# K, V and the first two contexts of cross attention are computed inside the last bodies of self attention

## The chip, the cores and the metric

The kernel runs on one core of a Trainium2 chip. The time is device microseconds (us) of one execution of the whole program. The program has three phases one after the other: self attention, cross attention, MLP. Each phase is a block of its own with its own semaphores; at the end of a block all engines meet at a barrier.

## The reference

```python
x_norm = modulate(_ln(x), shift_a, scale_a)          # x: (16, 224, 512)
q, k, v = split(x_norm @ W_qkv + b_qkv)              # 16 heads of 32
attn_out = softmax(q k^T * scale) v @ W_proj + b_proj
x = x + gate_a * attn_out
q_c = _ln(x) @ W_qc + b_qc
k_c, v_c = split(_ln(context) @ W_kvc + b_kvc)       # context: (16, 750, 512)
x = x + (softmax(q_c k_c^T * scale) v_c) @ W_cproj + b_cproj
x_norm2 = modulate(_ln(x), shift_m, scale_m)
x = x + gate_m * (gelu(x_norm2 @ W_mlp1 + b_mlp1) @ W_mlp2 + b_mlp2)
```

`k_c` and `v_c` depend only on the context and on W_kvc, so they need nothing of self attention.

## The kernel before, in words

Every product of the projections is made of three float32r matmuls (high times low, low times high, high times high; `product`, L71 to L73), so each operand is kept as a high part, rounded by ScalarE (ACT), and a low part, the difference, made by VectorE (DVE).

**Self attention** works through one batch of 16 after the other. `bodies` calls `body` with c = 0 to 18, and each engine has its own `body`, a loop over 16 steps h, one for each head. Body c computes the attention of batch c, and between its heads the filling work of the table `FILL`: K, Q, V of batch c+1, the output projection ("p") of batch c-1, the cross query ("c") of batch c-2 and transposes ("tx", "ty"). A head's second scores, its exponentials and its part of P·V come six heads late (`LAG`). Body 15 is the last with heads of its own and has no K, Q or V to fill with; body 16 finishes the heads of batch 15 and its output projection; body 17 turns the last x for the cross query, and its last product runs at the start of body 18. The row maxima of four heads are turned by TensorE (PE, L473), split by DVE (L708, L710) and written by a DMA of SyncE (SP, `place_maxima`, L301) as two more rows of the stacked Q; only then may the second scores (L485) of these heads run. Behind body 18 SP waits for all stores of `x1` and `qc`, and the barrier follows.

In body 14 SP loads W_kvc (`load_wkv`), in body 15 ACT and DVE split it (`high_wkv` L875, `low_wkv` L679), and SP loads context 0 into `c_in`, whose statistics DVE takes at the end of body 15 (L683). ACT normalizes it in body 16 (L879).

**Cross attention** first has a stretch of its own: six tiles of context 0 are transposed (L1336) and split (L1615, L1504), then `FIRST`: eight halves of K (four groups of four heads, each in two halves of 376 and 374 keys) and six tiles of V, with the six tiles of context 1 between the V. K is copied by SP into `kst` (`stack_k` L1270: twelve DMAs a group; three rows of parts, high, low, high), and `qc` into `qst` (`load_q` L1263: three DMAs a group). GpSimd (POOL) fills the two rows of ones of `kst` with one MEMSET (L1706). Then come the scores of head 0 (L1375) and bodies 0 to 16, made like those of self attention, with K and V of batch c+1 and the tiles of context c+2 as filling. The second scores are L1389, six heads late and again behind `place_maxima` (L1278). SP's order in front of body 0 is: Q and K of the four groups, six tiles of context 2, then the maxima of group 0.

Each engine runs its instructions in the order in which they are written; nothing is scheduled. A wait stands in the engine's own queue and holds up all behind it.

## Time and profile before

| | |
|---|---|
| median of 3 runs | 2712.4 us (2710.79 to 2716.66) |
| profiled execution | 2714.79 us, its span 2712.8 us |
| PE busy | 2616.2 us, 96% |
| DVE, ACT, POOL busy | 63%, 42%, 48% |
| PE's mean granted clock | 0.978 |
| body 15 begins, about | 678 us |
| last product of self attention ends | 760.3 us |
| first PE instruction of cross attention | 768.0 us |
| scores of cross head 0 | 812.2 us |
| first second scores of cross attention | 831.5 us |
| MLP begins, about | 1945 us |

The span runs from the first to the last instruction that the profiler recorded. A row of a timeline has the start in us, the duration in us, the engine, the line and the operation with its output and inputs; what stands in brackets is how long the engine had been idle before, and what ended that. The granted clock ("PEclk") is the share of TensorE's full speed (2.4 GHz) that was granted in a stretch: 1.00 is all of it, 0.50 is 1.2 GHz throughout.

### The profile page before, as it was taken

The numbers are of one execution on the slowest core, as the hardware profiler recorded it, in microseconds if no ns is written. First come the engines' busy times: TensorE is split into PE (matmuls) and PEld (weight loads), VectorE is DVE, ScalarE is ACT, GpSimd is POOL, SyncE is SP. The second block draws the span as 40 slices with busy tenths as digits, with TensorE's granted clock in tenths as the row PEclk, the third lists the DMA queues.
The fourth block names the chain that finished last, engine by engine and source line by source line (L and its number), as shares of the span: only waits on it lengthen the run. The fifth ranks groups of instructions, "written<-read, shape, count | busy, mean of one in ns | idle before, by whom it ended". The sixth has DMA issues, their size and how long they took to land. (4 is left out here: it accounts for less than half of the span.)

```text
span 2712.8 us, 49884 instructions
## 1 busy us (share of the span) xinstructions
PE 2616.2 (96%) x18548; PEld 2150.8 (79%) x18548; DVE 1708.4 (63%) x3413; ACT 1126.3 (42%) x2187; POOL 1303.5 (48%) x1447
## 2 busy tenths in 40 slices
PE   8899999999789999999999999999799999999997
PEld 6688888888578888888888888887478888888886
DVE  6677777776727777777777777776654444444431
ACT  4354444444434555555555555554432212212210
POOL 1445445454415777777777777767611221220211
PEclk9999999999889999999999999999799999999999
DMA  7454545545243444444444444334231111111110
GB/s 221 127 131 118 130 124 137 129 117 153 85 131 98 113 113 112 109 112 113 118 113 111 111 120 117 107 89 124 83 113 36 43 47 36 43 47 36 43 43 24
DMA packets 190609, 269.86 MB, mean 99 GB/s; under 512 B 32769, under 2 KB 110593, under 8 KB 190353
## 3 DMA queue, kind: packets, MB, share of 16 engines
q1 hardware_dynamic: 187296, 259.33, 35.4%
q0 software_dynamic: 3072, 7.34, 0.8%
q8 instruction: 149, 2.44, 0.4%
q14 instruction: 92, 0.75, 0.1%
HBM read 111.11 MB, written 36.77 MB: 55 GB/s over the span
## 5 line engine op out<-in xcount | busy, mean ns | idle before, releaser
L1639 ACT ACTIVATE cross_prT<-cross_tr_ps 125x448 f32<-125x448 f32 x768 | 407.4, 544 | 285.0 <-PE cross_tr_ps L1389 275.9
L1517 DVE TENSOR_REDUCE cross_parts<-cross_sc_ps 112x1 f32<-112x500 f32 x512 | 336.9, 664 | 213.3 <-PE cross_sc_ps L1375 212.0
L1690 POOL TENSOR_TENSOR cross_part<-cross_prT 125x448 f32<-125x448 f32 x252 | 291.7, 1157 | 212.8 <-PE cross_or_ps L1409 113.7
L1013 POOL TENSOR_TENSOR self_psum<-self_prT 112x224 f32<-112x224 f32 x256 | 180.9, 707 | 331.0 <-ACT self_prT L903 321.0
L1389 PE MATMUL cross_tr_ps<-cross_qst,cross_kst 98*125 98x224 f32 x1536 | 312.7, 287 | 3.8 <-ACT cross_prT L1639 3.3
L1389 PEld LDWEIGHTS cross_tr_ps<-cross_qst,cross_kst 98*125 98x125 f32 x1536 | 256.7, 189 | 62.0 <-ACT cross_prT L1639 23.3
L1692 POOL TENSOR_TENSOR cross_part<-cross_part,cross_prT 125x448 f32<-125x448 f32 x252 | 291.5, 1157 | 19.8
L2087 ACT ACTIVATE mlp_hv<-mlp_h_ps,mlp_b 128x512 f32<-128x512 f32 x112 | 76.9, 687 | 520.1 <-PE mlp_h_ps L73 506.1
L1375 PE MATMUL cross_sc_ps<-cross_kst,cross_qst 96*112 96x500 f32 (+1 forms) x1024 | 262.6, 337 | 3.2 <-DVE cross_parts L1517 3.0
L2004 DVE CAST mlp_hT_h<-mlp_hv 128x512 fp32r<-128x512 f32 x112 | 53.4, 477 | 320.0 <-ACT mlp_hv L2087 320.0
L903 ACT ACTIVATE self_prT<-self_st_ps 112x448 f32<-112x448 f32 x256 | 138.2, 541 | 187.3 <-PE self_st_ps L485 186.9
L1375 PEld LDWEIGHTS cross_sc_ps<-cross_kst,cross_qst 96*112 96x112 f32 x1024 | 164.2, 178 | 19.0 <-DVE cross_parts L1517 4.3
L1694 POOL TENSOR_TENSOR cross_psum<-cross_part 125x224 f32<-125x224 f32 x252 | 169.8, 674 | 19.7
L71 PE MATMUL mlp_a_ps<-mlp_w_l,mlp_hT_h 128*128 128x512 f32 x448 | 178.3, 398 | 0.0
L701 DVE TENSOR_REDUCE self_nmax<-self_sc_ps 112x2 f32<-112x448 f32 x256 | 154.4, 613 | 36.9 <-PE self_sc_ps L456 36.9
L72 PE MATMUL mlp_h_ps<-mlp_xT_h,mlp_w_l 128*128 128x512 f32 x448 | 177.5, 396 | 0.0
L72 PE MATMUL mlp_a_ps<-mlp_w_h,mlp_hT_l 128*128 128x512 f32 x448 | 176.9, 395 | 0.0
L1402 PE MATMUL cross_or_ps<-cross_prT,cross_vt 125*32 125x224 f32 x3072 | 167.5, 369 | 9.7 <-DVE cross_ou L1548 9.0
L73 PE MATMUL mlp_h_ps<-mlp_xT_h,mlp_w_h 128*128 128x512 f32 x448 | 176.7, 395 | 0.0
L73 PE MATMUL mlp_a_ps<-mlp_w_h,mlp_hT_h 128*128 128x512 f32 x448 | 176.6, 394 | 0.0
L71 PE MATMUL mlp_h_ps<-mlp_xT_l,mlp_w_h 128*128 128x512 f32 x448 | 176.6, 394 | 0.0
L1519 DVE TENSOR_REDUCE cross_parts<-cross_sc_ps 112x2 f32<-112x500 f32 x256 | 170.2, 665 | 0.0
(274 smaller groups left out, 6742.2 us busy)
## 6 DMA issues: line engine op xcount, KB each, us to landing
cross_kst<-cross_nat_h SPq DMA_DIRECT2D x512, 93.8 KB, 2.2
cross_c_in<-in_context SPq DMA_DIRECT2D x96, 250.0 KB
cross_kst<-cross_nat_l SPq DMA_DIRECT2D x256, 93.8 KB, 2.2
cross_qst<-qc SPq DMA_DIRECT2D x192, 112.0 KB, 2.5
self_kst<-self_nat_h SPq DMA_DIRECT2D x128, 112.0 KB, 2.3
self_qst<-self_natq_h SPq DMA_DIRECT2D x128, 112.0 KB, 3.0
self_x_in<-in_x SPq DMA_DIRECT2D x16, 448.0 KB, 3.8
self_kst<-self_nat_l SPq DMA_DIRECT2D x64, 112.0 KB, 2.3
```

Source lines behind the costliest of these rows:

```text
L71: pe.matmul(out, lhs[0], rhs[1], start=first, stop=False)
L72: pe.matmul(out, lhs[1], rhs[0], start=False, stop=False)
L73: return pe.matmul(out, lhs[0], rhs[0], start=False, stop=last)
L1013: pool.tensor_tensor(psum[:, j], prT[:, j, 0], prT[:, j, 1], ALU.add).then_inc(p_summed, 1)
L1375: last = pe.matmul(sc_ps[u][0:QN, at:at + cn], qst[0:TERMS * HD, g, j, t * QN:(t + 1) * QN], kst[0:TERMS * HD, g, j, c0:c0 + cn], start=Tr ...
L1389: last = pe.matmul(bank(h, c)[0:SN, m * N:(m + 1) * N], kst[:, g, j, kt * SN:(kt + 1) * SN], qst[:, g, j, :], start=True, stop=True)
L1517: dve.tensor_reduce(parts[:, g % 2, j, u, 0:1], sc_ps[u][0:QN, 0:SHALF[0]], AX_X, ALU.max, negate=True).then_inc(maxed, 1)
L1519: dve.tensor_reduce(parts[:, g % 2, j, :, 1], sc_ps[u][0:QN, 0:QT * SHALF[1]].rearrange("p (t k) -> p t k", t=QT), AX_X, ALU.max, negate=T ...
L1639: act.activation(prT[:, slot(h), 2 * c:2 * c + 2], bank(h, c)[0:SN, 0:2 * N].rearrange("p (k t) -> p k t", k=2), ACT.Exp).then_inc(exped, 1)
L1690: pool.tensor_tensor(part[:], prT[:, j, 0:2], prT[:, j, 2:4], ALU.add).then_inc(pre_summed, 1)
L1692: pool.tensor_tensor(part[:], part[:], prT[:, j, 4:6], ALU.add).then_inc(pre_summed, 1)
L1694: pool.tensor_tensor(psum[:, j], part[:, 0], part[:, 1], ALU.add).then_inc(p_summed, 1)
```

## The change

The work between the barrier and head 0 is taken out of cross attention and written into the bodies 15, 16 and 17 of self attention. A `Seam` object holds the buffers and semaphores that both phases share; the buffers are laid over self attention's own ones that are no longer used, and cross attention and MLP place theirs by the class `Room`. New positions:

- body 14: SP loads context 0, in two DMAs of three tiles, before the store of x1; W_kvc behind the last maxima.
- body 15: DVE takes the statistics of context 0 at h = 0, 1, 2 (L806), POOL inverts at h = 3, ACT normalizes at h = 4, 5, 6 (L1030); six tiles are transposed at h = 6, 7, 8 (L643, split at L1038 and L824), V of tiles 0 and 1 at h = 9 and 10; ACT issues the load of context 1 at h = 8. The output projection at h = 10 waits for V's bank.
- body 16: V of tiles 2 to 5 at h = 0 to 3, K halves 0 and 1 at h = 7 and 8, 2 and 3 at h = 12, 4 to 6 at h = 13 to 15. SP stacks Q and K of group 0 (`stack_first`) when two halves of K are there.
- body 17: K half 7 at h = 0, six tiles of context 1 at h = 1 and 2, ACT issues the load of context 2 at h = 3.
- cross attention begins with the scores of head 0; SP stacks groups 1, 2 and 3 first. The wait for the stores of x1 and qc stands in cross attention now. The MEMSET of ones has become sixteen, behind that wait.

The cross bodies and the MLP have the same work in the same order.

```diff
+def stack_first(eng, seam, qc, g, kst, qst, k_done, q_done):
+    for r, s in enumerate((0, 0, 1)):
+        src = qc[0, s, g * P:(g + 1) * P].rearrange("(j d) t -> d j t", d=HD)
+        eng.dma_start(qst[HD * r:HD * r + HD].bitcast(F32), src).then_inc(q_done, 16)
+    for j in range(HPG):
+        for r, s in enumerate((0, 1, 0)):
+            eng.dma_start(kst[j][HD * r:HD * r + HD].bitcast(F32), seam.nat[s][HD * j:HD * j + HD, g].bitcast(F32)).then_inc(k_done, 16)
...
+        TILES_AT, V_AT, LATE_V_AT = {6: (0, 1), 7: (2, 3), 8: (4, 5)}, {9: 0, 10: 1}, {0: 2, 1: 3, 2: 4, 3: 5}
+        K_AT = {(0, 7): (0,), (0, 8): (1,), (0, 12): (2, 3), (0, 13): (4,), (0, 14): (5,), (0, 15): (6,), (1, 0): (7,)}
+        NEXT_TILES_AT = {1: (0, 1, 2), 2: (3, 4, 5)}
...
+        def v_bank_free(t):
+            return (seam.cT_l, 5 + t) if t < 2 else (maxed, B * NH) if t < 4 else (seam.v_done, t - 1)
+        def k_bank_free(i):
+            return (seam.v_done, 5 + i) if i < 2 else (seam.k_l, i - 1)
...
                 if b.c == B - 2:
-                    load_wkv()
+                    sp.wait_ge(v_ps, 2 * B)
+                    load_context()
+                if b.c == B:
+                    sp.wait_ge(sum_ps, KC * B)
+                    sp.wait_ge(seam.k_l, 2)
+                    stack_first(sp, seam, qc, 0, [seam.kst[:, j] for j in range(HPG)], seam.qst, seam.k_stacked, seam.q_stacked)
                 if prv:
                     store_x1(z)
                 if att:
                     place_maxima(b, 3)
+                if b.c == B - 2:
+                    load_wkv()
...
             bodies(body)
-            sp.wait_ge(x1_out, 32 * B)
-            sp.wait_ge(qc_out, 32 * B)
...
+                if part == 0 and kind == "p" and o.c == B - 2:
+                    pe.wait_ge(seam.v_done, c + 1)
...
+            def cross_v(t):
+                pe.wait_ge(*v_bank_free(t))
+                pe.wait_ge(seam.cT_l, t + 1)
+                for k in range(KC):
+                    if t == 0:
+                        pe.wait_ge(wkv_l, k + 1)
+                    last = product(pe, v_bank(t)[0:SN, 0:H], ...)
...
+                    if b.c == B - 1 and h in (4, 5, 6):
+                        for t in range(2 * (h - 4), 2 * (h - 3)):
+                            normalize_context(0, t)
+                    for t in TILES_AT.get(h, ()) if b.c == B - 1 else ():
+                        high_context(0, t)
+                    if b.c == B - 1 and h == 8:
+                        load_next_context(1)
+                    if b.c == B - 1 and h in V_AT:
+                        keep_v(V_AT[h])
...
@@ cross attention, SP @@
-            sp.dma_start(bkv[:], b_kvc_t).then_inc(columns_in, 16)
-            load_q(Batch(0), 0)
-            for t in range(ST):
-                load_c(Batch(1), t)
-            load_q(Batch(0), 1)
-            for g in range(KC):
+            sp.wait_ge(seam.x1_out, 32 * B)
+            stack_first(sp, seam, qc, 1, kst[1], qst[1], k_stacked[1], q_stacked[1])
+            for g in range(2, KC):
+                if g == 3:
+                    sp.wait_ge(seam.qc_out, 32 * B)
+                load_q(Batch(0), g)
                 stack_k(Batch(0), g)
-                if g + 2 < KC:
-                    load_q(Batch(0), g + 2)
-            for t in range(ST):
-                load_c(Batch(2), t)
             bodies(sp, body)
@@ cross attention, PE @@
-            for t in range(ST):
-                fill_(Batch(-2), ("c", t))
-            for i, f in enumerate(FIRST):
-                fill_(Batch(-1), f)
-                for t in FIRST_TILES.get(i, ()):
-                    fill_(Batch(-1), ("c", t))
             for u in range(3):
                 score(Batch(0), 0, u)
```

**ScalarE in body 15, h = 4 to 8.** L875 and L1026 are the casts of W_kvc, L903 and L1083 the exponentials of a head, L914 and L1094 casts of the turned x, L909 and L1089 the high part of the attention output. Before:

```order
L914 CAST self_yT_h<-self_tx_ps 128x448 [waits self_yT_ps,self_c_ps]
L875 CAST cross_wkv_h<-cross_wkv_raw 128x1024 [waits self_wkv_in0]
L903 ACTIVATE self_prT<-self_st_ps 112x448 [waits self_pv_done,self_p_summed,self_turned]
L914 CAST self_yT_h<-self_tx_ps 128x448 [waits self_yT_ps,self_c_ps]
L909 ACTIVATE self_oT_h<-self_ou,self_bqkv 128x224 [waits self_o_done]
L875 CAST cross_wkv_h<-cross_wkv_raw 128x1024 [waits self_wkv_in1]
L903 ACTIVATE self_prT<-self_st_ps 112x448 [waits self_pv_done,self_p_summed,self_turned]
L875 CAST cross_wkv_h<-cross_wkv_raw 128x1024 [waits self_wkv_in2]
L903 ACTIVATE self_prT<-self_st_ps 112x448 [waits self_pv_done,self_p_summed,self_turned]
```

The same stretch of the change, in which L1030 normalizes context tiles:

```order
L1026 CAST cross_wkv_h<-cross_wkv_raw 128x1024 [waits self_wkv_in0]
L1030 ACTIVATE cross_c_in<-cross_c_in,self_nm_c,self_rs_c 125x512 [waits self_nmr_c] x2
L1083 ACTIVATE self_prT<-self_st_ps 112x448 [waits self_pv_done,self_p_summed,self_turned]
L1094 CAST self_yT_h<-self_tx_ps 128x448 [waits self_yT_ps,self_c_ps]
L1089 ACTIVATE self_oT_h<-self_ou,self_bqkv 128x224 [waits self_o_done]
L1026 CAST cross_wkv_h<-cross_wkv_raw 128x1024 [waits self_wkv_in1]
L1030 ACTIVATE cross_c_in<-cross_c_in,self_nm_c,self_rs_c 125x512 [waits self_nmr_c] x2
L1083 ACTIVATE self_prT<-self_st_ps 112x448 [waits self_pv_done,self_p_summed,self_turned]
L1026 CAST cross_wkv_h<-cross_wkv_raw 128x1024 [waits self_wkv_in2]
L1030 ACTIVATE cross_c_in<-cross_c_in,self_nm_c,self_rs_c 125x512 [waits self_nmr_c] x2
```

The first pair of normalizations, with its wait for `nmr_c`, now stands between the first cast of W_kvc and the exponential of head 15 of batch 14.

**SyncE at the start of cross attention.** L1263 loads Q, L1253 a tile of context, L1270 stacks K of a group, L1278 writes the row maxima. Before, from the barrier on (left out are the rest of the twelve stacking DMAs of each group, and groups 2 and 3):

```order
L1248 UNCONDITIONAL_BRANCH [waits barrier_Pool_Activation_PE_DVE_SP_release]
L1307 DMA cross_bkv<-in_b_kvc_t 128x8
L1263 DMA cross_qst<-qc 32x4x224 x3
L1253 DMA cross_c_in<-in_context 125x512 [waits self_first_q1] x6
L1263 DMA cross_qst<-qc 32x4x224 x3
L1270 DMA cross_kst<-cross_nat_h 32x750 [waits self_m_h]
...
L1253 DMA cross_c_in<-in_context 125x512 [waits self_first_q1] x6
L1278 DMA cross_qst<-cross_mrow_h 1x8x112 [waits self_x1_out]
L1278 DMA cross_qst<-cross_mrow_l 1x8x112
```

(Cross attention's semaphores bear the names of self attention's here, whose places they took: `self_m_h` is its count of K halves, `self_x1_out` that of its split maxima, and in the piece below that is `self_constant`.) Of the change, where L137 and L1463 load Q, L140 and L1470 stack K, and L1478 writes the maxima:

```order
L1446 UNCONDITIONAL_BRANCH [waits barrier_Pool_Activation_PE_DVE_SP_release]
L137 DMA cross_qst_14119<-qc 32x4x224 [waits shared_x1_out]
L137 DMA cross_qst_14119<-qc 32x4x224 x2
L140 DMA cross_kst_14116<-cross_nat_h 32x750
...
L1463 DMA cross_qst_14114<-qc 32x4x224 x3
L1470 DMA cross_kst_14117<-cross_nat_h 32x750 [waits shared_k_l]
...
L1463 DMA cross_qst_14115<-qc 32x4x224 [waits shared_qc_out]
L1463 DMA cross_qst_14115<-qc 32x4x224 x2
L1470 DMA cross_kst_14120<-cross_nat_h 32x750 [waits shared_k_l]
...
L1478 DMA cross_qst_69<-cross_mrow_h 1x8x112 [waits self_constant]
L1478 DMA cross_qst_69<-cross_mrow_l 1x8x112
```

The maxima of group 0 stand behind 45 DMAs that are issued from the start of the phase on. Before, 60 DMAs of Q and K and twelve of context tiles stood ahead of them, but the scores of head 0 came only near their end; now they are the first work of PE.

## Rows read from the trace of the kernel before

**Rows 1.** Busy time of each engine by stretch, body 15 to head 0
```profile
678.00:698.00 20.00, 11.69 (x102) 8.17 (x101) 17.43 (x33) 11.70 (x20) 8.93 (x11) 0.87 0.26 88
698.00:717.00 19.00, 19.00 (x148) 15.07 (x147) 15.52 (x29) 5.65 (x12) 10.12 (x11) 0.87 0.34 102
717.00:731.00 14.00, 8.89 (x67) 5.37 (x66) 8.07 (x24) 9.32 (x17) 6.60 (x10) 0.61 0.37 114
731.00:738.40 7.40, 7.07 (x26) 4.81 (x27) 2.98 (x4) 1.90 (x3) 1.69 (x2) 0.81 0.02 6
738.40:768.00 29.60, 15.57 (x105) 14.60 (x104) 6.78 (x17) 5.72 (x12) 4.39 (x6) 0.77 0.24 78
768.00:779.00 11.00, 9.90 (x40) 8.87 (x41) 4.16 (x7) 3.87 (x7) 10.06 (x1) 0.54 0.36 112
779.00:812.20 33.20, 33.20 (x179) 29.52 (x177) 11.82 (x28) 14.08 (x25) 2.09 (x4) 1.00 0.66 168
```

**Rows 2.** The same view, the cross bodies up to the MLP
```profile
831.50:1945.00 1113.50, 1096.10 (x8887) 905.27 (x8887) 811.30 (x1492) 600.90 (x1150) 815.44 (x871) 0.99 0.41 111
```

**Rows 3.** Timeline of PE, one half of K and one tile of V, to the next's start
```profile
780.40 0.33 PE L71 MATMUL cross_sc_ps<-cross_cT_l,cross_wkv_h 128*128 128x376 f32 x1
782.45 0.34 PE L71 MATMUL cross_even_ps<-cross_cT_l,cross_wkv_h 128*128 128x374 f32 x1
...
792.78 0.39 PE L71 MATMUL cross_sc_ps<-cross_wkv_l,cross_cT_h 128*125 128x512 f32 x1
795.58 0.39 PE L71 MATMUL cross_even_ps<-cross_wkv_l,cross_cT_h 128*125 128x512 f32 x1
```

**Rows 4.** Timeline of DVE in body 15
```profile
690.15 0.39 DVE L718 TENSOR_TENSOR self_ou<-self_or_ps,self_rb 128x224 f32<-128x224 f32 x1
...
699.31 1.21 DVE L679 TENSOR_TENSOR cross_wkv_l<-cross_wkv_raw,cross_wkv_h 128x1024 fp32r<-128x1024 f32 x1
```

**Rows 5.** Operations by tile: shapes that the change moves (ns min/median/max)
```profile
L683 DVE BATCH_NORM_STATS2 self_st_c<-cross_c_in x6: 672/682/689, 701.3 to 715.1; 125x6 f32<-125x512 f32 x6
L1504 DVE TENSOR_TENSOR cross_cT_l<-cross_tr_ps,cross_cT_h x12: 669/679/681, 769.7 to 813.1; 128x500 fp32r<-128x500 f32 x12
L1615 ACT CAST cross_cT_h<-cross_tr_ps x12: 577/581/599, 769.1 to 812.4; 128x500 fp32r<-128x500 f32 x12
L879 ACT ACTIVATE cross_c_in<-cross_c_in,self_nm_c,self_rs_c x6: 797/799/815, 725.5 to 734.1; 125x512 f32<-125x512 f32 x6
```

**Rows 6.** Timeline of ACT in body 15
```profile
688.77 0.55 ACT L903 ACTIVATE self_prT<-self_st_ps 112x448 f32<-112x448 f32 x1
```

**Rows 7.** Timeline of PE at the places that the sum runs through
```profile
697.72 0.71 PE L485 MATMUL self_st_ps<-self_qst,self_kst 98*112 98x224 f32 x2 [1.44 <-DMA self_qst<-self_mrow_l]
698.23 0.63 PE L71 MATMUL self_pj_ps<-self_wproj_l,self_oT_h 128*112 128x512 f32 x1
703.74 0.39 PE L71 MATMUL self_pj_ps<-self_wproj_l,self_oT_h 128*112 128x512 f32 x1
...
747.36 0.87 PE L419 MATMUL self_tx_ps<-shared_ident,self_x_res 112*128 112x112 f32 x4 [3.59 <-ACT self_x_res L871]
768.01 1.27 PE L1336 MATMUL cross_tr_ps<-shared_ident,cross_c_in 125*128 125x125 f32 x5 [7.68 <-PEq L98]
812.16 0.91 PE L1375 MATMUL cross_sc_ps<-cross_kst,cross_qst 96*112 96x500 f32 x4
831.47 0.67 PE L1389 MATMUL cross_tr_ps<-cross_qst,cross_kst 98*125 98x224 f32 x4
```

**Rows 8.** DMAs issued by SP
```profile
767.97 0.36 SPq L1307 DMA_DIRECT2D cross_bkv<-in_b_kvc_t  x1
789.48 1.54 SPq L1263 DMA_DIRECT2D cross_qst<-qc  x3
799.31 1.55 SPq L1263 DMA_DIRECT2D cross_qst<-qc  x3
```

**Rows 9.** What SP's queue waited for, 755 to 870 us
```profile
SPq L410 <- DMA qc<-self_natq_l: 3.2, 1, 3.2
```

More of the change, by code:

```diff
@@ L583, in body @@
                         fill(b, *f)
+                    if b.c == B - 1 and h in V_AT:
+                        cross_v(V_AT[h])
+                    if b.c == B and h in LATE_V_AT:
+                        cross_v(LATE_V_AT[h])
+                    for i in K_AT.get((b.c - B, h), ()):
+                        cross_k(i)
                     if b.c == 1 and h in (13, 14):
@@ L742, in body @@
                         evict(*f)
+                    for i in K_AT.get((b.c - B, h), ()):
+                        low_k(i)
                     for _, c, _, o in fills(b, h, ("tx",)):
@@ L946, in body @@
                         evict(*f)
+                    for i in K_AT.get((b.c - B, h), ()):
+                        high_k(i)
                     for _, c, _, o in fills(b, h, ("ty",)):
@@ L1100, in cross_phase @@
-        mrow = [sb(f"mrow_{s}", [HPG * QT, QN], F32R) for s in "hl"]
-        rb = sb("rb", [P, N])
-        st = sb("st", [SN, ST, 6])
-        turn = sb("turn", [1, 1])
-        mv = sb("mv", [SN, ST, 2])
-        ve, rs, nm = sb("ve", [SN, ST]), sb("rs", [SN, ST]), sb("nm", [SN, ST])
+        bkv, cT, nat = seam.bkv, seam.cT, seam.nat
+        low = Room(nc, "cross", low_at, seam.x_at)
+        prT = low.take("prT", [SN, HPG + 1, ST, N])
+        late = [low.take(f"qst{g}", [ROWS, HPG, N], F32R) for g in (2, 3)]
@@ new lines, in cross_phase @@
+        middle = Room(nc, "cross", seam.x_at + 4 * KC * S, seam.free_at)
+        kst = [seam.kst] + [middle.take(f"kst{g}", [ROWS, HPG, S], F32R) for g in (1, 2)]
+        kst = [[k[:, j] for j in range(HPG)] for k in kst]
+        psum = middle.take("psum", [SN, HPG + 1, N])
+        qst = [seam.qst, seam.room.take("qst1", [ROWS, HPG, N], F32R), *late]
+        fourth = [seam.room.take(f"kst3{j}", [ROWS, S], F32R) for j in range(3)]
+        spare = Room(nc, "cross", seam.kst_at + 4 * KC * S, seam.nat_at[0])
@@ new lines, in cross_phase @@
+        fourth.append(spare.take("kst33", [ROWS, S], F32R))
+        kst.append([k[:] for k in fourth])
+        rb = spare.take("rb", [P, N])
+        small = Room(nc, "cross", seam.qst_at + 4 * ST * H, seam.nat_at[1])
+        ou = small.take("ou", [P, 2, N])
+        part = small.take("part", [SN, 2, N])
+        mrow = [spare.take("mrow_h", [HPG * QT, QN], F32R), small.take("mrow_l", [HPG * QT, QN], F32R)]
+        parts = small.take("parts", [QN, 2, HPG, QT, 2])
+        nmax = small.take("nmax", [QN, 2, HPG * QT])
@@ L1107, in cross_phase @@
+        turn = small.take("turn", [1, 1])
+        top = Room(nc, "cross", seam.qst_end, SBUF_END)
+        vt = [seam.vt, top.take("vt1", [SN, ST, H])]
+        ones = top.take("ones", [SN, HD])
+        st, mv = top.take("st", [SN, ST, 6]), top.take("mv", [SN, ST, 2])
+        ve, rs, nm = top.take("ve", [SN, ST]), top.take("rs", [SN, ST]), top.take("nm", [SN, ST])
         sc_ps = [ps(f"sc_ps{u}") for u in range(3)]
@@ L1478, in stats @@
             def stats(b, t):
-                wait(dve, c_loaded[t], b.n(16, 0))
+                if b.c == 2:
+                    dve.wait_ge(seam.c_loaded[t // 3], 48)
+                else:
+                    dve.wait_ge(c_loaded[t], here(b).n(16, 0))
                 dve.bn_stats(st[:, t], c_in[:, t]).then_inc(stats_done, 1)
@@ new lines, in mlp_phase @@
+        turn = middle.take("turn", [1, 1])
+        st, mv = middle.take("st", [P, GT, 6]), middle.take("mv", [P, GT, 2])
+        ve, rs, nm = middle.take("ve", [P, GT]), middle.take("rs", [P, GT]), middle.take("nm", [P, GT])
+        xT = [Room(nc, "mlp", seam.kst_at + 4 * MLP, seam.nat_at[0]).take("xT_h", [P, KC, GN], F32R)]
+        high = Room(nc, "mlp", seam.nat_at[0] + 4 * MLP, seam.nat_at[1])
+        xT.append(high.take("xT_l", [P, KC, GN], F32R))
+        hT = [high.take(f"hT_{s}", [P, GR, GN], F32R) for s in "hl"]
@@ L1748, in mlp_phase @@
+        top = Room(nc, "mlp", seam.nat_at[1] + 4 * MLP, SBUF_END)
+        gate = top.take("gate", [P, 2, H])
+        oT = [top.take(f"oT_{s}", [P, KC, P], F32R) for s in "hl"]
+        x_in, b2, hv = top.take("x_in", [P, H]), top.take("b2", [P, H]), top.take("hv", [P, GN])
         h_ps = [ps(f"h_ps{i}") for i in range(2)]
```

332 lines of the change are left out of this document (201 added, 131 removed).

## Prediction

> **What bounds the kernel now.** I read the table of busy time by stretch first. Over the cross bodies PE works 1096.1 of 1113.5 us [rows 2]; none of that work changes, nor does the MLP's. So only the stretch from body 15 to the first cross head can change, 678 to 812.2 us, and the few us behind the barrier. There the same view by stages [rows 1] is what the reader should look at. PE is busy 105.3 of 134.2 us: it idles 8.3 us in the first half of body 15, 5.1 in body 16, 14.0 between 738.4 and 768. And its granted clock is 0.87, 0.61, 0.77 and 0.54 in those stretches, 1.00 only from 779 on. Taking (1 minus the clock) times PE's busy time in each row for work done at 1.2 instead of 2.4 GHz, some 17 us more are lost. So about 46 us of these 134 are waste, and the change moves work into the places where the waste is. That is its chance. Whether it is taken depends on what bounds there, so the second view is each engine's timeline in body 15. DVE is busy 17.43 of 20 us from 678 to 698 [rows 1] and stands without a gap around its reciprocals [rows 4]; PE's 8.3 us of idle time are waits for what DVE and ACT make of the attention. Body 15 is bound by the side engines, not by PE. The tail behind 738.4 is bound by the chain normalise, turn, split, multiply (PE waits 3.59 us for ACT at 747.36 [rows 7]), with little work beside it. The third view is SP's queue, which matters for the first cross heads.
>
> **The work moved.** Six V tiles by 2.80 us (792.78 to 795.58) are 16.8 us, eight K halves by 2.05 us (780.40 to 782.45) 16.4 us [rows 3]. The twelve turned tiles cost PE some 0.6 us each, about 7 us: in 779 to 812.2 PE was full with 33.2 us [rows 1], which these products alone fill. Where work lands in a hole it is free, where it lands in a full or waiting stretch it costs its length, and more at the low clock.
>
> **Body 15, h = 0 to 8.** DVE gets here six statistics at 0.68 us and six low parts of turned tiles at 0.68 [rows 5], 8.2 us, and four small steps, 0.7: some 8.9 us on an engine that had 2.6 us of idle time in 20. (The statistics stood at 701.3 to 715.1 before, so they only come earlier; for h = 0 to 8 they are added.) ACT gets six normalizations at 0.80, six casts at 0.58 [rows 5], the copies of V, and two DMA issues: about 10 us, where it was busy 11.70 of 20 [rows 1]. ACT has the room, but not the order. The order shows that the first two normalizations stand ahead of the exponential of head 15 of the batch before, with the wait for `nmr_c`. Its chain is six statistics at h = 0 to 2, the aggregate, POOL's two steps, and DVE's last factor, which stands in DVE's queue behind the reciprocal and `self_ou` of 690.15 [rows 4], and everything ahead of it is later by the added DVE work. I place it at about 693.4; two normalizations follow, so the exponential that ran at 688.77 [rows 6] runs at about 695. That delays P·V of this head, its output, its high and low parts and then the output projection. Behind it comes DVE's last low part of W_kvc, 699.31 to 700.5 before [rows 4]: with the rest of the 8.9 us and a wait for the turned tiles I get 710.5 to 711.7. V of tile 0 needs that and the last tile's low part, so it starts about 712.4; at half clock it takes twice 2.80 less the share that was not PE's, about 5.1 us. The output projection of h = 10, at 698.23 before [rows 7], waits for V's bank (`v_done`): 718.2, 20 us later. The bounds: below, DVE's own 8.9 us and V's 2.8, so +12, if nothing queues up behind the wait; above +22. I take +20 because each link of the chain stands in one queue with the next.
>
> The rest of the body has less waiting: V of tile 1 is 2.8 us, and the clock may have recovered, since the same product took 0.63 us at 698.23 and 0.39 us at 703.74 [rows 7], which I credit with 1.7 us. The end of body 15 moves from about 717 to 738, +21.
>
> **Body 16.** V of tiles 2 to 5 (11.2 us) and K halves 0 and 1 (4.1 us) come to 15.3 us. From 717 to 738.4 PE idled 5.4 us and ran at 0.61 and 0.81 of full clock [rows 1]. The added work fills the 5.4; but the normalization for the projection stands behind the low parts of K on DVE, which I price at 2.9 us. Sum: +21 + 15.3 − 5.4 + 2.9 = +34 less about 1 us of clock: the mark 738.4 goes to about 771.3, +33.
>
> **The tail.** Before, 738.4 to 760.3 is 21.9 us with long waits. Six K halves (12.3 us) and the six tiles of context 1 and their splits (5.5 us with what waits for them) are 17.8 us. If they filled the waits, the tail would stay 21.9 plus what doesn't fit. But they stand at h = 12 to 15 and behind it, while the last cross query needs DVE's low parts of the last x, which queue behind those of K and of the tiles. Going through the queues I get 36.2 us at full clock and 39 at half: the end at 807.5 to 810.3 instead of 760.3.
>
> **The barrier.** SP waited 3.2 us for the last store of qc ahead of it [rows 9], which is part of the 7.68 us that PE stood [rows 7]. This wait goes into the next phase; 4.6 us are left. The first cross scores are at 812 to 815, mid 813.5, against 812.16 [rows 7]: +1.3.
>
> **Behind the barrier.** This I take for the surest cost. SP must issue three groups of Q and K, 45 DMAs, ahead of the maxima of group 0. Its pace is a group of 15 in 9.83 us (789.48 to 799.31) [rows 8], so the maxima are issued about 28 to 29.5 us after the start, and land about a microsecond and a half later (PE waited 1.44 us for such a DMA at 697.72 [rows 7]). PE wants them 19.3 us after the first scores (812.16 to 831.47) [rows 7]. Before, SP had done its groups while PE still made K and V. So PE waits about 11 us. Then, having waited and run thin before, it runs at 1.2 GHz for a while: as at 698.23, and in 768 to 779 at 0.54 [rows 1]; I take +3 (the stretch at 698 to 703.7, 0.24 us lost on each 0.39, some twelve products). The sixteen MEMSETs on POOL, in place of one of 10.06 us [rows 1], cost nothing by +19. If they cost more each than by size, they end by +25 at most and hide behind SP. The context loads that moved add no wait that I can name: the DMA engines are busy at 0.26 to 0.37 in body 15 and 16 [rows 1].
>
> Here the Trainium skill speaks against me. "DMA: Bandwidth & Descriptors", section "Issuing engines are not separate DMA queues", says that spreading DMAs over issuing engines saves only the sequencer's time, mostly small beside the transfer itself. By that the length of SP's queue is not what decides, the maxima come in time, and of the sum +4 is left (rival E). The row is against it so far: SP is at it for 9.83 us a group [rows 8], while the 16 DMA engines are busy at 0.66 in 779 to 812.2 [rows 1].
>
> The skill's "TensorE: Matmul & The Clock Gate", section "HAM oscillation — how this bites in real kernels", has an engine that waits over and over start at the low clock each time. My schedule adds waits to body 15; by that rule V of tile 1 too would be 2.8 us longer there, and the sum +18 and not +15. The granted clock of 0.87 in a stretch with 8.3 us of idle time [rows 1] does not show it that strongly.
>
> **Sum.** +1.3 + 11 + 3 = +15.3 on the profiled execution's 2714.8 is 2730; that lies 2.4 above the median of 2712.4, so I forecast 2727.
>
> **The rivals.**
>
> A, the forecast, slower by 15: 0.55. Its own range: 2716 (body 15 moves by 14 and the clock holds) to 2740 (39 us of tail, stacks at a slower pace).
>
> B, about the same or a bit slower: the side chain in body 15 costs only its DVE work, +12 instead of +20, and body 16 and the tail pass on nothing of that. Head 0 then comes at about 804, −8, and the +14 behind the barrier leave +3 to +7. For it: PE's work at full clock is only some 88 of the 134.2 us. Against it: DVE has 2.6 us of room [rows 1]. 0.12.
>
> C, faster: PE is the bound after all once the work is there, the clock stays high because it no longer idles, and half of the 46 us of waste is regained. Head 0 at 790, −22, with +14 gives −8: about 2704. It decides where the regained waste exceeds 14 + 5.4 = 19.4 us. For it: V and K need nothing of self attention, and 14.0 us of idle time in the tail [rows 1] are filled by 17.8 us of work. Against: my chains end late for the side engines' sake. 0.18. If also SP's queue is no cost, it is −22: 2690, which I leave out.
>
> E, SP's queue is no limit: the maxima need not wait for the 45 DMAs' full pace, the term of 11 goes. +1.3 and the 3 of clock, +4: 2716. For it: from the barrier on nothing else uses the DMA engines; against it the pace of 9.83 us a group. 0.05.
>
> D, worse, +30: the waits of V's bank and of the tiles cross each other in body 15, and P·V of all heads behind is held. 2742. 0.10.
>
> Faster by over 0.2% (5.4 us, about what a measurement of this kernel tells from no change): C, with a little of B, 0.20. Within 0.2%: E and most of B, 0.14. Slower: A, D and the rest, 0.66. The range that should hold 8 of 10 goes from 2702 to 2741.
>
> **What the profile after would show.** PE's first cross scores at 812 to 815, the first second scores 30 us behind them, not 19.3, with an idle time released by the DMA of `mrow`; SP issuing without a pause between. In body 15, ACT idle ahead of the first L1030, and V of tile 0 at about 712. PE's clock at 0.5 to 0.6 from 700 to 715. If head 0 comes before 800, the sum over body 15 is wrong; if PE reaches the second scores 20 us after it, the term of SP is.

## The result and the profile after

The changed kernel takes 2730.5 us (median of 4 runs, 2727.7 to 2732.7), the kernel before 2713.0 us in the same session: a ratio of 1.0061 (95% interval 1.0048 to 1.0073), 17.6 us slower by the medians. The forecast was 2727, slower by 15. The profiled execution has a span of 2730.9 us, 18.1 more than the 2712.8 of before. Direction, size and the two largest terms came as predicted, but the sum is this near partly by luck: the stretch up to the first cross scores came out 6.2 us longer than predicted, and 3.0 us came back far behind, in stretches whose work the change does not touch. Two executions of the experiments below, one of 8623 us (mean granted clock 0.41) and one of 2890 us (0.84), are left out of the medians.

First the busy time by stretch of the changed kernel; the columns are those of [rows 1], the last row is for the cross bodies as [rows 2].

```profile
678.00:698.00 20.00, 8.28 (x58) 5.77 (x56) 14.30 (x35) 7.68 (x14) 6.33 (x9) 0.69 0.63 188
698.00:717.00 19.00, 13.21 (x69) 10.27 (x70) 13.90 (x21) 11.97 (x21) 3.74 (x5) 0.59 0.20 58
717.00:731.00 14.00, 13.65 (x80) 10.00 (x79) 2.39 (x6) 2.71 (x5) 2.13 (x4) 0.90 0.23 84
731.00:738.40 7.40, 6.70 (x73) 5.81 (x72) 7.30 (x13) 2.68 (x6) 6.84 (x7) 1.00 0.18 53
738.40:768.00 29.60, 26.37 (x159) 20.89 (x158) 12.28 (x32) 14.36 (x26) 7.21 (x11) 0.88 0.19 58
768.00:779.00 11.00, 8.52 (x34) 7.00 (x35) 3.16 (x5) 0.94 (x2) 4.11 (x4) 0.84 0.62 149
779.00:819.60 40.60, 29.45 (x186) 27.67 (x184) 13.55 (x29) 11.97 (x24) 1.97 (x3) 0.82 0.24 84
819.60:850.00 30.40, 20.44 (x101) 19.15 (x101) 18.56 (x38) 3.42 (x6) 11.76 (x18) 0.84 0.62 159
831.50:1963.50 1132.00, 1104.87 (x8936) 913.93 (x8934) 821.40 (x1514) 602.00 (x1151) 816.91 (x873) 0.99 0.42 112
```

The waste is where it was, and more of it. In 678 to 717 PE idles 17.5 us (8.3 before) at a clock of 0.69 and 0.59. From 717 to 768 it is busy 46.7 of 51 us, where it had been busy 31.5: the added V and K do fill the holes there, as hoped for. From 779 on come two stretches with 11 and 10 us of idle time. Behind 850 PE first runs some microseconds at half clock. These two rows are the same product of a V tile, in the kernel before and in the changed one, where it is the first one of V that runs at full clock again:

```profile
835.38 0.40 PE L71 MATMUL cross_even_ps<-cross_wkv_l,cross_cT_h 128*125 128x512 f32 x1
856.48 0.40 PE L71 MATMUL cross_even_ps<-cross_wkv_l,cross_cT_h 128*125 128x512 f32 x1
```

Here the changed kernel is 21.1 us late. It still is at 1800 us, and only 18.1 of it are left at the end; the part on why the prediction was right comes back to this.

The waits of PE over this region, in the changed kernel (engine, line, what it waited for: us in total, times, the longest):

```profile
PE self_st_ps L570 <- DMA self_qst<-self_mrow_l: 9.7, 2, 8.9
PE cross_tr_ps L1579 <- DMA cross_qst<-cross_mrow_l: 9.2, 1, 9.2
PE cross_sc_ps L1565 <- PEq L98: 4.5, 1, 4.5
PE self_tx_ps L504 <- DVE self_yT_l L796: 3.8, 3, 1.5
PE self_pj_ps L643 <- DVE cross_cT_l L824: 3.3, 2, 2.4
PE self_pj_ps L71 <- DVE self_oT_l L791: 2.9, 1, 2.9
PE self_sc_ps L643 <- DVE cross_cT_l L824: 2.8, 2, 2.2
PE self_pj_ps L71 <- DVE cross_cT_l L824: 2.1, 1, 2.1
```

The second and third lines are the two terms that were predicted (11, measured 9.2; 4.6, measured 4.5). The first was not in the prediction at all. And PE's timeline at the places that the sum runs through, against [rows 7]:

```profile
687.33 0.71 PE L570 MATMUL self_st_ps<-self_qst,self_kst 98*112 98x224 f32 x2 [8.87 <-DMA self_qst<-self_mrow_l]
...
713.70 0.79 PE L71 MATMUL self_pj_ps<-cross_wkv_l,cross_cT_h 128*125 128x512 f32 x1 [2.06 <-DVE cross_cT_l L824]
714.28 0.63 PE L72 MATMUL self_pj_ps<-cross_wkv_h,cross_cT_l 128*125 128x512 f32 x1
...
719.90 0.46 PE L71 MATMUL self_pj_ps<-self_wproj_l,self_oT_h 128*112 128x512 f32 x1 [0.35 <-issue]
...
807.54 0.53 PE L71 MATMUL self_pj_ps<-self_yT_l,self_wqc_h 128*128 128x224 f32 x1 [1.43 <-DVE self_yT_l L796]
...
819.67 0.73 PE L1565 MATMUL cross_sc_ps<-cross_kst,cross_qst 96*112 96x500 f32 x1 [4.47 <-PEq L98]
...
850.09 1.15 PE L1579 MATMUL cross_tr_ps<-cross_qst,cross_kst 98*125 98x224 f32 x4 [9.20 <-DMA cross_qst<-cross_mrow_l]
```

V of tile 0 starts at 713.70 (predicted 712.4), runs at half clock (0.63 a product, 5.48 us in all, predicted 5.1), and the output projection that was at 698.23 is at 719.90 (predicted 718.2). The first cross scores are at 819.67 (predicted 813.5; 812.16 before), the first second scores 30.4 us behind them (predicted 30; 19.3 before).

SP behind the barrier, in the changed kernel (start, duration of the issue):

```profile
819.48 1.50 SPq L137 DMA_DIRECT2D cross_qst<-qc  x3
...
828.57 2.18 SPq L1463 DMA_DIRECT2D cross_qst<-qc  x3
...
838.34 1.56 SPq L1463 DMA_DIRECT2D cross_qst<-qc  x3
...
847.47 0.69 SPq L1478 DMA_DIRECT2D cross_qst<-cross_mrow_h  x1
848.20 0.65 SPq L1478 DMA_DIRECT2D cross_qst<-cross_mrow_l  x1
```

Three groups of 9.1, 9.8 and 9.1 us without a pause, then the maxima, 28.0 us after the start.

### The profile page after: what moved, and what is told of

It reads as the page before. It is cut to its first block and busy times, and to the rows that moved or that the text cites. A ratio compares the mean times of both kernels' runs of the same rounds, so it can differ in the third digit from the quotient of the medians.

```text
span 2730.9 us, 49894 instructions
## 1 busy us (share of the span) xinstructions
PE 2616.8 (96%) x18548; PEld 2155.8 (79%) x18548; DVE 1709.2 (63%) x3411; ACT 1127.0 (41%) x2187; POOL 1304.1 (48%) x1460
## 5 line engine op out<-in xcount | busy, mean ns | idle before, releaser
L1083 ACT ACTIVATE self_prT<-self_st_ps 112x448 f32<-112x448 f32 x256 | 138.6, 542 | 191.7 <-PE self_st_ps L570 191.5
```

## The experiments

Two groups of causes had to be told apart: what holds the maxima of cross attention (the issue queue or the transfers), and what in body 15 costs what (the unforeseen wait of 8.87 us, the work for context 0 on the side engines, or the order in their queues). After that I tried to make the idea of the change pay. The first four experiments, the next four and the last three were measured in a session each, in which the kernel before took 2714.0, 2713.1 and 2713.8 us, against 2713.0 in that of the result. So a difference between kernels of two sessions is uncertain by about 1 us beyond the scatter of the runs.

**Maxima of group 0 ahead of group 3.**

```diff
                 if g == 3:
+                    place_maxima(Batch(0), 0)
                     sp.wait_ge(seam.qc_out, 32 * B)
```

> SP writes the maxima of group 0 between the stacking of group 2 and that of group 3, so behind 30 DMAs and not 45. Theory (the 9.20 us that PE waited at 850.09 are the issue time of SP's queue): 30 DMAs take some 19.7 us, the wait falls to 0 to 1 us, and PE does not start slow afterwards; the kernel gains 9 to 12 us, about 2720. Rival (the transfers limit, as the Trainium skill's page DMA: Bandwidth & Descriptors would have it, or K of group 3 becomes the late one): the wait moves to head 12 or stays, gain under 3 us.

Measured: 2718.9 us (10 runs), ratio to before 1.0016 (1.0006 to 1.0025): 11.6 us less than the changed kernel. PE's first second scores in that kernel:

```profile
839.71 0.66 PE L1580 MATMUL cross_tr_ps<-cross_qst,cross_kst 98*125 98x224 f32 x4 [0.23 <-DMA cross_qst<-cross_mrow_l]
```

SP's queue around the maxima:

```profile
837.10 0.69 SPq L1478 DMA_DIRECT2D cross_qst<-cross_mrow_h  x1
837.83 0.65 SPq L1478 DMA_DIRECT2D cross_qst<-cross_mrow_l  x1
838.53 1.38 SPq L1463 DMA_DIRECT2D cross_qst<-qc  x3
```

The wait is 0.23 us instead of 9.20, the distance from the first scores (818.36 there) is 21.4 us, and the four products take 0.66 us (1.15 in the changed kernel). The same DMAs are issued, only in another order, so it was the queue. K of group 3 comes 1.4 us later and nobody waits for it.

**The load of context 0 in other rows.** The trace of the changed kernel showed what stood in the way of the maxima in body 15. These are the two lines of the DMA view from 668 to 682, busy tenths of the 16 DMA engines and GB/s in 40 slices:

```profile
DMA  2000521333333389753333369743333468999999
GB/s 57 0 10 0 47 18 35 82 123 123 129 123 135 129 240 328 246 193 129 117 129 123 117 211 304 252 181 117 127 123 121 140 181 334 304 263 269 228 205 240
```

Where only the context load runs, the engines are busy at 0.3 and move 120 to 135 GB/s; the peaks are x1's store. A tile of context has 125 rows; other tiles here have 112 or 128.

```diff
                 for half in range(2):
-                    sp.dma_start(c_in[:, 3 * half:3 * half + 3], ...).then_inc(c_loaded[half], 16)
+                    for lo, hi in ((0, 112), (112, SN)):
+                        sp.dma_start(c_in[lo:hi, 3 * half:3 * half + 3], src[lo:hi]).then_inc(c_loaded[half], 16)
```

(and the same for the two loads that ScalarE issues)

> Each load of three context tiles made of two DMAs, of 112 and of 13 rows, in place of one of 125 rows; same bytes. Theory (the 8.87 us that PE waited for the maxima at 687.33 are the context load: it runs at some 125 GB/s and a DMA busy share of 0.3, so it holds a part of the 16 engines for 12 us, and the maxima's small pieces queue up behind it): the load lands in 5 to 6 us, the wait goes to under 1 us, V of tile 0 starts at about 706 instead of 713.7, gain 6 to 8 us, about 2723. Rival (the chain of DVE and ACT sets the time of V of tile 0, the wait for the maxima lies beside it): the wait goes, V starts at 712 as before, gain under 2 us. Second rival (row count has nothing to do with the rate): the wait stays at 9 us.

Measured: 2724.8 us (5 runs), 5.7 less than the changed kernel. The DMA view of the same stretch:

```profile
DMA  9682000924899999997999999998842100951799
GB/s 197 164 187 54 0 10 0 111 53 117 293 421 380 281 269 293 269 105 117 240 281 263 275 228 275 340 263 275 293 176 76 51 12 10 94 47 70 328 410 410
```

and V of tile 0:

```profile
710.65 0.79 PE L71 MATMUL self_pj_ps<-cross_wkv_l,cross_cT_h 128*125 128x512 f32 x1 [2.06 <-DVE cross_cT_l L825]
```

The rate is mostly 230 to 420 GB/s and the load over before 679; the wait for the maxima is 0.71 us. Two executions can lie a microsecond apart as a whole, so V is counted from SP's issue of these maxima (676.69 in the changed kernel, 677.61 here): 37.0 us before the edit, 33.0 with it. That is 4.0 us and not 8: half of the wait lay beside the chain of the side engines, so theory and first rival are each half right. The rest of what this profile gains is the clock: from V's start to the first cross scores (713.70 to 819.67, here 710.65 to 813.16) it is 102.5 us instead of 106.0, with a granted clock of 1.00 from 717 to 780 (0.90 in the changed kernel). That the edit brings this level about is not shown; the last section has two kernels with the same waits at either level.

**Both edits.** (The two diffs above together.)

> Both edits together. If the two waits are independent, the gains add: 15 to 20 us off 2730.5, about 2712, level with the kernel before. If the tail between them takes up what body 15 gives back, it is no better than the first edit alone, about 2720.

Measured: 2717.3 us (10 runs), ratio to before 1.0008 (0.9998 to 1.0017). The gains do not add: 13.2 and not 17.3 us, though a part of these 4 us may be the scatter of the medians (the runs of this kernel go from 2711.7 to 2720.0). V starts at 709.09, but its way to the first scores (815.25) is 106.2 us again: the clock level that the profile of the edit alone had is not there in this one.

**The load issued by ScalarE.**

In ScalarE's body, with the two DMAs as they were; SyncE's are gone:

```diff
+                    if b.c == B - 2 and h == 12:
+                        load_context()
```

> The load of context 0 is issued by ScalarE at h = 12 of body 14, at about the same time as SP issued it, whole 125 rows as in the changed kernel. Theory that the maxima are held in SP's own ring behind the context's pieces: they are free of them now, the wait of 8.87 us falls to 2 us or less and the kernel gains 5 to 8 us. Rival, that the engines themselves are taken, whoever issues (what the Trainium skill's page DMA: Bandwidth & Descriptors states in its section on issuing engines): the wait stays at 7 to 9 us and the time at 2729 to 2731.

Measured: 2727.8 us (3 runs), 2.7 less than the changed kernel; the ratio to before is 1.0049 (1.0032 to 1.0065), whose interval overlaps the changed kernel's. The wait fell to 5.17 us, which fits neither text: the theory had 2 us or less, the rival 7 to 9. From the issue of the maxima to PE's start it is 6.9 us here (675.18 to 682.12), 10.6 in the changed kernel (676.69 to 687.33) and 2.5 in both_edits (676.05 to 678.51). A part of the gain may be that the load was issued 9.4 us ahead of the maxima here and 8.4 in the changed kernel; what the other queue gave beyond that is not shown. The maxima have another queue than the context now and are still late: in this the Trainium skill's section "Issuing engines are not separate DMA queues" (page "DMA: Bandwidth & Descriptors") agrees with the run. In the first experiment it does not help, since there the sequencer's issue time of 45 DMAs was the thing, which the same section counts as small.

The next three stand on both_edits.

**Normalizations one head later.**

```diff
-                    if b.c == B - 1 and h in (4, 5, 6):
+                    if b.c == B - 1 and h in (5, 6, 7):
```

> On top of both_edits: ScalarE normalizes the tiles of context 0 at h = 5, 6, 7 of body 15 instead of 4, 5, 6, so the exponential of head 15 of the batch before no longer stands behind the wait for the factor. The prediction's step: that order delays this exponential by 6 us and with it P times V, the output and all behind. If it is a link of the chain that ends in V of tile 0, PE's wait of 2.25 us for the exponential goes and V starts 1 to 2 us earlier, gain 1 to 2 us on 2717.3. Rival: the chain runs through the normalizations themselves, they come later now, V starts at the same time or 1 us later; no gain.

Measured: 2716.0 us (10 runs), 1.4 less than both_edits, within the scatter. V of tile 0 is at 708.06; counted from PE's second scores behind the maxima at body 15's start (679.45) that is 28.6 us, against 30.6 in both_edits (678.51 to 709.09). So the step predicted, the exponential behind the factor, is a link of the chain, and worth 2 us of the 20.

**Context 0 raw.**

```diff
-                        stats_context(0, 2 * h)
-                        stats_context(0, 2 * h + 1)
...
-                            normalize_context(0, t)
```

> On top of both_edits, context 0 is not normalized: its six statistics, the aggregation, the two steps of GpSimd, the factor and the six normalizations are left out, the tiles are turned as loaded. This takes 4.7 us from VectorE and 4.7 us from ScalarE in body 15. If the side engines' work for context 0 is what makes V of tile 0 late (my 20 us, as it was predicted), V starts 5 to 9 us earlier than in both_edits and the kernel gains 4 to 8 us. Rival: the tiles' path (turn, round, subtract, bank free, 3.3 us a pair) and the low parts of W_kvc set it; then V comes at most 2 us earlier.

Measured: 2713.2 us (10 runs), 4.1 less than both_edits. V of tile 0 is 25.2 us behind the mark (679.45 to 704.63), 5.4 us earlier. So even without all of the added statistics and normalizations V comes late. What holds it then is on ScalarE's timeline of this kernel:

```profile
702.89 0.48 ACT L1086 ACTIVATE self_oT_h<-self_ou,self_bqkv 128x224 fp32r<-128x224 f32 x1 [3.77 <-DVE self_ou L856]
...
703.28 0.56 ACT L1034 CAST cross_cT_h<-self_pj_ps 128x500 fp32r<-128x500 f32 x1
...
703.73 0.57 ACT L1034 CAST cross_cT_h<-self_pj_ps 128x500 fp32r<-128x500 f32 x1
```

ScalarE stands 3.77 us for the attention output, and the rounding of the last two tiles, which PE had turned by 701.8, is queued behind it. The changed kernel has the same: 3.56 us at 711.95, then the two casts, then V.

**The tail in another order.**

```diff
-        K_AT = {... (0, 15): (6,), (1, 0): (7,)}
-        NEXT_TILES_AT = {1: (0, 1, 2), 2: (3, 4, 5)}
+        K_AT = {... (0, 15): (6,), (1, 5): (7,)}
+        NEXT_TILES_AT = {6: (0, 1), 13: (2, 3), 14: (4, 5)}
...
-                    if prv and h == 15:
+                    if prv and h == (14 if b.c == B else 15):
                         stats(z, y, ...)
...
-                    if b.c == B + 1 and h == 3:
+                    if b.c == B + 1 and h == 15:
                         load_next_context(2)
```

> On top of both_edits: the statistics of the last y are taken before the low part of K half 5 (h = 14) instead of behind that of half 6 (h = 15), K half 7 stands between the two turns of the last x, the six tiles of context 1 stand behind these turns and between the last cross query products. Theory (the tail's idle time, 6.8 us of waits between 790 and 807 in the changed kernel and some 3 us of slow clock after them, comes from the order, not from the amount of work): 5 to 8 us gained, about 2711, below the kernel before. Rival: each turned tile waits for its split on the side engines wherever it stands, so the waits move with the tiles; gain under 2 us.

Measured: 2710.7 us (10 runs), ratio to before 0.9989 (0.9980 to 0.9999), 6.6 less than both_edits. PE's waits from 760 to 860 us in both_edits, of over 1.5 us and without the barrier's 4.5:

```profile
PE self_pj_ps L71 <- DVE self_oT_l L792: 2.9, 1, 2.9
PE self_sc_ps L644 <- DVE cross_cT_l L825: 2.8, 2, 2.2
PE self_tx_ps L505 <- DVE self_yT_l L797: 2.4, 1, 2.4
```

and in this kernel:

```profile
PE self_tx_ps L505 <- ACT self_x_res L1023: 3.4, 1, 3.4
PE self_pj_ps L71 <- DVE self_oT_l L792: 2.9, 1, 2.9
```

With the smaller ones (1.4 and 1.0 us in the first, 0.2 in the second) the first are 10.5 us, the second 6.5: the waits do not move with the tiles, so it was the order. Which of the three moves gave how much was not taken apart.

**V 0 and V 1 in body 16 too** (on top of tail_rearranged; the two tiles also take other banks there).

```diff
-        TILES_AT, V_AT, LATE_V_AT = {...}, {9: 0, 10: 1}, {0: 2, 1: 3, 2: 4, 3: 5}
+        TILES_AT, V_AT, LATE_V_AT = {...}, {}, {0: 0, 1: 1, 2: 2, 3: 3, 4: 4, 5: 5}
...
                 if part == 0 and kind == "p" and o.c == B - 2:
-                    pe.wait_ge(seam.v_done, c + 1)
+                    pe.wait_ge(seam.cT_l, 5 + c)
```

> As tail_rearranged, and V of tiles 0 and 1 also moved from body 15 (h = 9, 10) to body 16, all six V at h = 0 to 5. The output projection of h = 10 then waits only for the split of the last tiles and not for V. V of tile 0 ran at half clock, 5.48 us for 2.8, after a wait of 2.06 us. Theory: the wait and the slow half of V 0 are saved, 3 to 5 us below tail_rearranged. Rival: without V the first products of the projection pay for the slow clock instead, and the six V in body 16 cost their full length there; within 1 us of tail_rearranged.

Measured: 2704.6 us (5 runs), ratio to before 0.9965 (0.9951 to 0.9979), 6.1 less than tail_rearranged and more than expected. The first cross scores are at 802.68.

**The split of the last tiles ahead of the output** (on top of the last, with the later normalizations). On ScalarE and VectorE the work on tiles 4 and 5 at h = 8 is written before that on the last part of the attention output.

> On top of tail_and_v_in_body16: the normalizations at h = 5 to 7 as in normalize_one_head_later, and at h = 8 ScalarE and VectorE split the last two turned tiles of context 0 before they make the last part of the attention output, not behind it. In all runs so far ScalarE stands 3.3 to 3.6 us ahead of that output with the two finished tiles behind it in its queue. Theory (a queue of one engine holds the tiles, not the work): the output projection starts 3 to 5 us earlier, gain 3 to 5 us on 2704.7. Rival: the projection waits for the low part of the output's third group instead, gain under 1.5 us.

Measured: 2702.3 us (5 runs), ratio to before 0.9959 (0.9945 to 0.9973): the lowest of all, 2.4 less than the last. ScalarE's rows:

```profile
704.08 0.58 ACT L1041 CAST cross_cT_h<-self_pj_ps 128x500 fp32r<-128x500 f32 x1 [1.04 <-PE self_pj_ps L644]
704.91 0.58 ACT L1041 CAST cross_cT_h<-self_pj_ps 128x500 fp32r<-128x500 f32 x1 [0.26 <-PE self_pj_ps L644]
708.19 0.48 ACT L1093 ACTIVATE self_oT_h<-self_ou,self_bqkv 128x224 fp32r<-128x224 f32 x1 [2.71 <-DVE self_ou L856]
```

The casts no longer stand behind the output, and the output projection starts 29.2 us behind SP's issue of the maxima (676.61 to 705.79) for 33.1 in the kernel of the last experiment (675.42 to 708.50), 3.9 us earlier as the theory had it. But PE now waits 3.09 us for an exponential at 710.88, which takes back a part. Two edits are in this number, and one of them, the later normalizations, had been worth 2.0 us at V. The kernels with 2 us between them are hardly told apart; both are clearly faster than the kernel before.

**K half 7 back ahead of the turn** (on top of split_before_output).

```diff
-        K_AT = {... (1, 5): (7,)}
-        NEXT_TILES_AT = {6: (0, 1), 13: (2, 3), 14: (4, 5)}
+        K_AT = {... (1, 0): (7,)}
+        NEXT_TILES_AT = {5: (0, 1), 6: (2,), 13: (3,), 14: (4, 5)}
```

> On top of split_before_output: K half 7 goes back ahead of the first turn of the last x, where PE waits 3.43 us for ScalarE, and the tiles of context 1 take its place between and behind the two turns (two at h = 5, one at 6, one at 13, two at 14). Theory: 2.05 us of the wait are filled, 1 to 2 us gained. Rival: the wait only moves to the place between the turns; no gain.

Measured: 2704.3 us (5 runs), 2.0 more than split_before_output, which the scatter covers. The wait for ScalarE is 3.02 instead of 3.43 us, and a new one of 2.01 us stands at the tiles. So there is no gain, as the rival had it.

**Maxima ahead of group 2** (on top of tail_filled; `place_maxima(Batch(0), 0)` at `g == 2` in place of `g == 3`).

> On top of tail_filled: SP writes the maxima of group 0 between the stacking of group 1 and of group 2. PE's wait of 1.0 to 1.4 us for them behind the barrier goes. Theory: 1 us gained if group 2 still lands before head 8 wants it at some 26 us. Rival: the maxima are not made before 15 us, SP stands until then and group 2 comes 4 us late: slower by 1 to 3 us.

Measured: 2710.9 us (10 runs), 6.6 more than tail_filled. SP's queue in that kernel:

```profile
813.08 0.59 SPq L140 DMA_DIRECT2D cross_kst<-cross_nat_h  x1
818.18 0.69 SPq L1484 DMA_DIRECT2D cross_qst<-cross_mrow_h  x1
```

SP stands from 813.7 to 818.2 because the maxima do not exist yet, and all behind it comes so much later; PE then idles 7.66 us at 832.09. The trace shows the way from one to the other. ScalarE may write the next K of a group (L1804) only when SP has copied the old one out; it stands 12.74 us, until 830.24, and the last DMA of group 2 landed at 830.15. DVE, idle for 8.32 us, goes on at 830.84 with the low part of this K and then with the maxima of the scores, whose bank PE waits for. The rival was right, at twice its price; that ScalarE is the one that waits first, it did not have.

## Why the prediction was right, and where it was not

*What bounds.* Right: body 15 is bound by the side engines, the tail by the chain of the last x. PE filled 717 to 768 and was then held by the same kinds of wait.

*Body 15, +20 at the output projection.* Measured +21.7 (698.23 to 719.90). The chain was the predicted one for the most part: without the unforeseen wait V starts at 710.65, against 712.4, and the exponential that was placed at about 695 runs at 697.83 with that wait; counted from the issue of the maxima (677.31 before) the prediction was 35.1 us, measured were 37.0 with that wait and 33.0 without. Of its links, the order of the exponential is worth 2.0 us and the work for context 0 as a whole 5.4 us. A link that the prediction only named ("its output, its high and low parts") is what holds V in the end: the last two tiles are queued behind the output on ScalarE and VectorE, and splitting them first, together with the later normalizations, brought the output projection 3.9 us forward. That the wait and the too long chain nearly cancel (+21.7 for +20) is luck.

One reading of the rows before was too simple. Of PE's 8.3 us of idle time from 678 to 698, 2.1 were waits for the DMA of the maxima and not for what DVE and ACT make; [rows 7] has one of them, 1.44 us at 697.72. This DMA was on the path before the change already.

*The DMA loads.* Wrong: "The context loads that moved add no wait that I can name". They added the longest but one, 8.87 us. I had read a mean DMA share of 0.26 to 0.37 [rows 1] as room, when it was the sign of a load that does not use more. That rate can be read in the kernel before, in the DMA view from 688 to 697, where the load of context 0 runs alone:

```profile
DMA  0000221151023333333353333333233332321000
GB/s 2 0 12 4 27 55 36 64 55 46 36 82 118 118 118 137 137 118 127 118 209 137 118 127 118 137 137 118 109 137 127 118 137 109 118 82 36 24 10 0
```

Undoing it by the split of the rows gave 5.7 of the 17.6 us.

*Body 16 and the tail.* The end of body 15's products was predicted 21 us later and is 23 us later (716.97 to 740.09). The mark 738.4 was predicted at 771.3 and came at 776.4; the end of self attention at 807.5 to 810.3 and came at 815.2. The mis-sized part is the clock: after waits of 1.40 and 1.45 us PE made K half 0 in 4.13 us for 2.05, after 2.86 us the projection at 0.63 a product, and after 1.43 us the last query in 7.65 us. I had counted half clock only for the first V and for one bound of the tail. These make up nearly all of the 6.2 us by which the head of the sum (+7.5, predicted +1.3) is off. The prediction had set the rule of the Trainium skill ("TensorE: Matmul & The Clock Gate", section "HAM oscillation — how this bites in real kernels": waits restart the engine at the low clock) against V of tile 1. There it did not hold, this V took 2.95 us; in the three places just named the trace agrees with it. But normalize_one_head_later passes the first of these places, with the same waits, at a granted clock of 1.00 (last section), so no time can be counted on from it.

*The barrier.* Right: 4.47 us are left, 4.6 predicted.

*Behind the barrier.* Right, in mechanism and size. The mechanism is shown by moving two DMAs in the queue. The wait is 9.20 us for 11, the distance 30.4 for 30, and the slow clock behind it costs 2.5 us for 3: from the second scores to the product at 835.38 it was 3.9 us, to that at 856.48 it is 6.4. The changed kernel has lost 13.6 us behind its first scores there, and 14 were predicted.

*Behind the first bodies.* The prediction had nothing for this: "none of that work changes, nor does the MLP's". Up to the product at 856.48 the change costs 21.1 us, where the sum had 15.3, but at the end of the profiled execution it is 18.1. Matching PE's products of the two traces one by one, the delay is 19.9 us in the last cross bodies, 22.3 at 2010 us behind a stretch of changing clock, and then shrinks by 4.2 us over the MLP's products, all at full clock. One of their six groups, before and after:

```profile
L72 PE MATMUL mlp_h_ps<-mlp_xT_h,mlp_w_l 128*128 128x512 f32 x448 | 177.5, 396 | 0.0
L72 PE MATMUL mlp_h_ps<-mlp_xT_h,mlp_w_l 128*128 128x512 f32 x448 | 175.8, 392 | 0.0
```

The MLP's products that take 199.9 us in the trace of the kernel before, from 2100 to 2300 us, take 198.7 in each of the twelve traces of kernels with the change, the changed one and the eleven experiments. The change did move the MLP's buffers (`Room`); but there is only one trace of the kernel before, so whether that is the cause or this execution was slower stays open. Either way the nearness of 15 to 17.6 owes about 3 us to something that was not foreseen.

*The rivals.* C (PE reclaims half of the waste) did not come, since the waits of the side engines came with the work. E failed by the first experiment. B's half of the chain (+12) did not come: even the raw context has V 5.4 us earlier only.

What stays open: how much of the 6.1 us of moving V 0 and V 1 is clock and how much is the wait; why some executions pass the tail at full clock (below); and the 4.2 us of the MLP.

## What to carry to other kernels

Moving independent work into another phase's bodies pays by the position in each engine's queue, not by PE's idle time: work that made the kernel 17.6 us slower in one order makes it 11.5 us faster in another. Between the two lie only orders and places within bodies 15 to 17 and behind the barrier, and the cut of the context loads into two DMAs. When a start-up stretch is removed, ask what the queues did under its cover; here SP's 45 DMAs had been free, and two of them had to go ahead of the last 15. Put moved work where the side engines idle (here body 16: DVE is busy 2.39 of 14 us from 717 to 731), and behind no wait that it doesn't need. And look at the far end too: a change of the buffers' places can reach phases whose work is the same, and one trace of the kernel before can't settle it.

## What was not expected of the hardware

A load of 125 rows, each of three pieces of 2 KB, moved mostly at 117 to 137 GB/s with the DMA engines busy at 0.3, from either issuing engine; the same bytes as 112 and 13 rows moved mostly at 230 to 420 GB/s, a part of it x1's store, with the engines busy at 0.9. The traces' packets say more: a packet of 2 KB takes 84 ns in both, but from 670 to 673 us in the changed kernel, where the 125 rows are nearly alone, 5.3 of them are under way at a time on average, and 14.2 from 670.5 to 673 with 112 rows. 2 KB in 84 ns is 24 GB/s, and five of them at a time give 122. So an estimate from these rows is that about five of the 16 engines work off the long load, at full pace each; which number of rows gives how many was not tried further. A transfer of few bytes behind such a load (7 KB of maxima, issued at 676.69 and 677.36) kept PE until 687.33.

The same work passes this part at either clock level. Below is the stretch 731 to 760 in both_edits and in normalize_one_head_later, whose work from V's start on is the same and which is one microsecond ahead there:

```profile
731.00:760.00 29.00, 25.46 (x168) 20.27 (x161) 13.34 (x35) 14.49 (x27) 9.70 (x14) 0.88 0.22 64
```

```profile
731.00:760.00 29.00, 23.75 (x162) 18.87 (x160) 14.54 (x35) 14.35 (x26) 8.10 (x12) 1.00 0.23 70
```

From V's start to the first cross scores it is 106.2 us in the first and 102.6 in the second, with the same waits. This is likely a part of why runs of one such kernel scatter (2710.1 to 2718.2 us for normalize_one_head_later). A difference of 2 us between two of them says little, and the profiled execution can be 4 us from the median (2711.7 for 2716.0 in this kernel).
